# A fused attention, FFN and linear-attention kernel: three edits at the two ends of its first FFN phase

## The reference, cut to what matters

```python
x = x + attn_a(layernorm(x))    # one causal head of width 128, with rope
x = x + ffn(layernorm(x))       # the first FFN
x = x + attn_b(layernorm(x))    # linear attention: 16 heads of width 64
x = x + ffn(layernorm(x))       # the second FFN, same weights

def ffn(x):                     # x_prev is x one token earlier
    xr = mu_r * x + (1 - mu_r) * x_prev
    xk = mu_k * x + (1 - mu_k) * x_prev
    r = sigmoid(xr @ W_r.T)
    k = relu(xk @ W_k.T) ** 2
    return r * (k @ W_v.T)
```

## Time and profile before

| what | us |
|---|---|
| median of the 3 runs | 851.22 |
| all runs | 851.21, 851.22, 853.79 |
| the profiled execution's own time | 855.38 |
| its span | 853.5 |
| attention phase, from the span's start | 0 to about 208.2 |
| first FFN | 208.4 to 251.4 |
| linear phase with the second FFN | 251.7 to the end |
| PE busy over the span | 802.7 (94%) |
| DVE, ACT, POOL busy | 550.5, 558.1, 563.0 |

### The profile page before, as it was taken

How to read it: one execution, slowest core, us unless ns; L and a number is a source line. 1 busy time by engine, 2 the same in 40 slices (tenths; PEclk the granted TensorE clock), 3 DMA queues, 4 the chain that set the end, 5 groups by cost and what they waited for, 6 DMA issues and landing times.

```text
span 853.5 us, 31084 instructions
## 1 busy us (share of the span) xinstructions
PE 802.7 (94%) x13187; PEld 695.4 (81%) x13187; DVE 550.5 (65%) x1267; ACT 558.1 (65%) x1171; POOL 563.0 (66%) x449
## 2 busy tenths in 40 slices
PE   5889999999979999999999999999999999998897
PEld 4668999898867879888888788798888887886786
DVE  4997667674863556656756655666566566674775
ACT  4656555555768667767776767676767767665664
POOL 4971211311528897797797887977977978778361
PEclk9999999999989999999999999999999999999999
DMA  4300000100000000000000000000000000000012
GB/s 142 113 1 20 26 20 8 26 19 11 17 2 1 4 2 2 4 3 3 3 4 3 2 3 3 4 3 3 4 3 3 3 3 3 3 3 3 3 37 62
DMA packets 20423, 12.36 MB, mean 14 GB/s; under 512 B 7872, under 2 KB 19008, under 8 KB 20288
## 3 DMA queue, kind: packets, MB, share of 16 engines
q1 hardware_dynamic: 20288, 10.39, 4.4%
HBM read 8.29 MB, written 2.10 MB: 12 GB/s over the span
## 4 chain that ended last, share of the span: by engine, by line
PE 51%; POOL 7%; ACT 6%; issue 3%; DVE 3%; ACTq 0%; POOLq 0%; DVEq 0%
PE la_ps L1488 8%; PE la_ps L1490 6%; PE la_ps L1489 6%; PE la_o_ps L1551 4%; PE la_o_ps L1567 4%; PE la_s_ps L1581 4%; PE la_ps L1598 3%; PE la_ps L1532 3%; POOL la_scale L2177 3%; ACT la_u_hi L1985 2%; PE la_ps L1519 2%; PE la_ps L1633 2%; PE la_ps L1635 2%; PE la_ps L1634 2%; ACT n_xn L2025 2%
## 5 line engine op out<-in xcount | busy, mean ns | idle before, releaser
L2145 POOL TENSOR_TENSOR la_coef<-la_ssk,lt_mhalf 128x32 f32<-128x32 f32 x16 | 87.1, 5441 | 71.5 <-DVE la_ssk L1815 71.5
L1488 PE MATMUL la_ps<-la_x_hi,w_hi 128*128 128x256 f32 x384 | 116.8, 304 | 1.9 <-ACT la_v L1955 1.0
L1489 PE MATMUL la_ps<-la_x_lo,w_hi 128*128 128x256 f32 x384 | 107.6, 280 | 0.2 <-issue 0.2
L1490 PE MATMUL la_ps<-la_x_hi,w_lo 128*128 128x256 f32 x384 | 107.7, 280 | 0.0
L2177 POOL TENSOR_TENSOR la_scale<-la_scale,lt_mhalf 128x32 f32<-128x32 f32 x16 | 97.4, 6085 | 6.7 <-DVE la_scale L1791 6.7
L1838 DVE TENSOR_TENSOR lt_state<-la_s_ps,la_faded 128x512 f32<-128x512 f32 x62 | 42.6, 686 | 69.8 <-PE la_o_ps L1567 51.9
L1488 PEld LDWEIGHTS la_ps<-la_x_hi,w_hi 128*128 128x128 f32 x384 | 72.4, 188 | 14.2 <-issue 6.2
L530 POOL CAST w_hi<-qkv_w_raw 128x256 fp32r<-128x256 f32 x20 | 7.9, 396 | 109.5 <-PE qkv_xt_ps L573 78.8
L1489 PEld LDWEIGHTS la_ps<-la_x_lo,w_hi 128*128 128x128 f32 x384 | 72.6, 189 | 0.8 <-issue 0.4
L600 PE MATMUL qkv_v_ps<-V,qkv_probsT 128*128 128x128 f32 x544 | 71.9, 278 | 1.0 <-ACT qkv_probsT L706 1.0
L1490 PEld LDWEIGHTS la_ps<-la_x_hi,w_lo 128*128 128x128 f32 x384 | 72.3, 188 | 0.0
(11 more groups left out here) (235 smaller groups left out, 2436.1 us busy)
## 6 DMA issues: line engine op xcount, KB each, us to landing
qkv_w_raw<-in_w SPq DMA_DIRECT2D x20, 128.0 KB, 2.2
X<-in_x SPq DMA_DIRECT2D x8, 256.0 KB, 3.2
out<-X SPq DMA_DIRECT2D x8, 256.0 KB, 2.3
qkv_cos<-in_cos SPq DMA_DIRECT2D x4, 256.0 KB, 3.0
qkv_sin<-in_sin SPq DMA_DIRECT2D x4, 256.0 KB, 3.9
lt_w_out<-in_w_out SPq DMA_DIRECT2D x4, 128.0 KB, 2.7
qkv_w<-in_w_qkv SPq DMA_DIRECT2D x1, 320.0 KB, 3.6
const<-in_const SPq DMA_DIRECT2D x1, 256.5 KB, 4.2
```

Source lines behind the costliest of these rows:

```text
L1488: eng.matmul(out, l_hi, r_hi, start=True, stop=False)
L1489: eng.matmul(out, l_hi, r_lo, start=False, stop=False)
L1490: return eng.matmul(out, l_lo, r_hi, start=False, stop=True)
L2145: eng.tensor_tensor(coef[:, :], ssk[:, :], mhalf[:, :], ALU.pow).then_inc(s["coef_step"], 1)
```

## The change

Three edits, and one that follows from them.

1. DVE computes the moments of groups 2 and 3 of the FFN in the attention phase, after the copies of query tiles 12 and 13 of row 1, and POOL their inverse roots after the weight split of tile 14. In the FFN phase these moments and roots are left out.
2. In slot 8 of the FFN PE computes the keys of group 7 first, then the values of group 6, and the receptance of group 7 last; ACT does `square(7)` ahead of `tanh(7)`.
3. The x of the linear phase's first step is turned in slot 8 of the FFN by PE, ahead of the values of group 7, into the bank `xt_ps[0]`. ACT copies it there, POOL forms its low part there. The new class `LinearInput` holds the three buffers and their semaphores.
4. The linear phase starts at step -1 in place of -2, its ring of banks has one job less, and its first ACT instruction writes `yT` in place of `beta`.

```diff
+FFN_MEASURED = 4
...
         def attend_gpsimd(eng):
...
                         tables.gpsimd_rates(eng)
+                    if b == B - 1 and n == SMALL + 6:
+                        for g in range(2, FFN_MEASURED):
+                            next_norm.inverse_roots(eng, Tile(0, g))
...
         def attend_vector(eng, low_part):
...
                         next_norm.first_normalized(eng)
+                    if b == B - 1 and 2 <= n - SMALL - 2 < FFN_MEASURED:
+                        eng.wait_ge(o_read, (B - 1) * NT + SMALL)
+                        next_norm.moments(eng, Tile(0, n - SMALL - 2))
...
+class LinearInput:
+    def __init__(self, sb, sem):
+        self.xT = sb("la_xT", [P, B * P])
+        self.x_hi = sb("la_x_hi", [P, 2, B * P], F32R)
+        self.x_lo = sb("la_x_lo", [P, 2, B * P], F32R)
+        self.full, self.xt_ready, self.hi_ready, self.xlo_ready = (
+            sem("la_" + n) for n in ("first_full", "xt_ready", "first_hi", "xlo_ready"))
...
 # ffn_phase, POOL
-                if exists(g.later(2)):
+                if exists(g.later(2)) and not has_been_measured(g.later(2)):
                     norm.inverse_roots(eng, g.later(2))
...
             run_slots(eng, slot)
+            eng.wait_ge(first_x.xt_ready, 1)
+            eng.wait_ge(first_x.hi_ready, 1)
+            eng.tensor_tensor(first_x.x_lo[:, 0, :], first_x.xT[:, :], first_x.x_hi[:, 0, :].bitcast(F32),
+                              ALU.subtract).then_inc(first_x.xlo_ready, 1)
...
 # ffn_phase, DVE
-                if exists(g.later(2)):
+                if exists(g.later(2)) and not has_been_measured(g.later(2)):
                     norm.moments(eng, g.later(2))
...
 # ffn_phase, ACT
-                if exists(g.later(-1)):
+                if g.off == GROUPS:
+                    square(g.later(-1))
+                    tanh(g.later(-1))
+                    eng.wait_ge(first_x.full, 1)
+                    eng.activation(first_x.xT[:, :], xt_ps[0][:, 0:B * P], ACT.Copy).then_inc(first_x.xt_ready, 1)
+                    eng.activation(first_x.x_hi[:, 0, :], xt_ps[0][:, 0:B * P], ACT.Copy).then_inc(first_x.hi_ready, 1)
+                elif exists(g.later(-1)):
                     tanh(g.later(-1))
                     square(g.later(-1))
...
 # ffn_phase, PE
+                if g.off == GROUPS:
+                    keys(g.later(-1))
+                    values(g.later(-2))
+                    receptance(g.later(-1))
+                    eng.wait_ge(xt_ready, GROUPS - 1)
+                    eng.wait_ge(next_norm.ready, B)
+                    for b in range(B):
+                        mm = eng.transpose(xt_ps[0][:, b * P:(b + 1) * P], next_norm.xn[:, 0, b * P:(b + 1) * P], ident)
+                    mm.then_inc(first_x.full, 1)
+                    return
...
 # linear_phase
-        STEPS = range(-2, NT + 1)
+        STEPS = range(-1, NT + 1)
...
-                written(eng, *turned(n - 2))
+                if n > 2:
+                    written(eng, *turned(n - 2))
                 norm.normalize(eng, Tile(0, n))
...
-            eng.activation(beta[:, 0:1], const[:, C_LEFT:C_LEFT + 1], ACT.Silu)
+            eng.activation(yT[:, 0:1], const[:, C_LEFT:C_LEFT + 1], ACT.Silu)
```

18 lines of the change are left out of this document (10 added, 8 removed).

## The result

| kernel | median of the runs (lowest to highest) | profiled execution: time, span, mean clock |
|---|---|---|
| before | 851.22 us (850.66 to 853.79, 4 runs) | 855.38, 853.5, 0.989 |
| changed | 845.41 us (844.06 to 846.98, 4 runs) | 844.06, 841.9, 0.996 |

The ratio of the changed kernel's time to the time before is 0.992, with a 95% interval of 0.9899 to 0.9941. That is 6.8 us by the ratio (5.0 to 8.6) and 5.8 us by the medians, where the forecast had 4.0. Measured twice more on other chips, the ratio was 0.9926 [0.9904, 0.9947] and 0.992 [0.9901, 0.9939], and the medians were 5.5 and 6.9 us apart.

A forecast was written before the change was run, and what follows sets the result against it. A chain of waits without slack from the linear phase's start, and PE's waits around the first FFN, were taken as the bound. -1.7 + 0.05 - 0.25 - 1.9, with 0.2 more, took 851.22 to 847.2 us; range 844.9 to 849.9.

The forecast's parts named there:

- Edit 1: FFN start: groups 2 and 3 normalized early, PE's waits go, group 4 normalized 1.65 us sooner; -1.7 us.
- The next bound: FFN: group 4's normalizing waits for POOL's roots behind group 2's low part, beginning near 221.15 where it was 222.79.
- The cost in attention: Moved moments fit into DVE's wait for the scores at tiles 12 and 13; cost 0, bounds 0 and +0.3 us.
- the contention: FFN start: DVE's eight normalizing tiles and POOL's low part of group 0 hinder each other; +0.05 us, bound 0.3.
- Edit 2: FFN end: PE waits 1.05 us for POOL's low part before the keys, the last values start sooner; -0.25 us.
- Edit 3: Linear phase start: keys begin 1.2 us into the block, not 3.08; -1.9 us if the clock falls, -3.4 if not.
- A fall that comes later than before: Linear phase start: a clock fall in the middle of the first keys gives up to 0.5 us more, 0.2 taken.
- Nothing behind the first power: Linear phase's later steps: every engine's list stays the same and all starts move together; no gain counted there.
- The profile's own distance to the median: Whole kernel: the profiled execution lies 4.16 us above the median, unexplained; the same difference was taken for the changed kernel.
- The clock does not fall: Rival at the barrier: PE's shorter rest keeps the clock up; -5.35 us, 845.9 us; chance 0.26.
- Absorbed in part: Rival: in the FFN only PE's listed waits go, in the linear phase half the gain; -1.75, 849.5 us; chance 0.20.
- Slower: Rival in the linear phase: the 16 steps mesh worse, 0.41 us lost per step giving about 854 us; chance 0.04.

The follow-up runs named there:

- no_moments: Changed kernel with the moments and roots of groups 2 and 3 back in the FFN: 848.26 us, ratio 0.9931 to the kernel before.
- only_moments: Kernel before with only the moments and roots of groups 2 and 3 moved into attention: 853.44 us, ratio 0.9989.
- no_order: Changed kernel with the old order in the last FFN slot (receptance, values, keys; tanh ahead of squares): 848.57 us, ratio 0.9942 to the kernel before.
- only_turn: Kernel before with only the linear phase's first x turned in the FFN: 850.47 us, ratio 0.9962.
- before_shift1: Kernel before with one unread multiplication of 16 columns ahead of the FFN's last keys: 852.75 us, ratio 0.9986.
- no_turn: Changed kernel without turning the linear phase's first x in the FFN: 851.78 us, ratio 0.9978 to the kernel before.
- before_again: Kernel before, unchanged, measured and profiled a second time: 853.43 us, ratio 0.9999.

## Why the prediction was right or wrong

**Edit 1** (-1.7, bounds -1.1 and -2.0): 1.57 us off the FFN, by no_moments and by only_moments alike. The next bound was the one named, POOL's roots of group 4 behind the low part of group 2. The cost in attention was 0. For the contention 0.05 was taken; POOL lost 0.08 on the low part, and DVE the rest, 0.97 for eight tiles, where nobody waited for it. The trace agrees with what the prediction cites from the Trainium skill, SBUF — State Buffer, Who interferes with whom, in that the two get in each other's way; the loss of a whole DVE tile by POOL, 0.27 us, was not seen. In the runs the 1.57 us hardly show, by 0.5 us in only_moments and not at all against no_moments: in only_moments' profile, with a fall of the clock behind it, the edit gave 1.03 us back, which the prediction had no term for.

**Edit 2** (-0.25, bounds 0 and -0.6): 0.22 us between no_order and the changed kernel, 0.56 alone. PE stood 0.89 us before the keys where 1.05 was worked out.

**Edit 3** (-1.9 if the clock falls, -3.4 if not): both numbers came out, each in its own executions. The start took 15.07 us on the mean of three old profiles; 13.17 with a fall is 1.9 less, 11.61 without is 3.5 less. The betas and keys began 0.19 and 0.80 us into the block, where 1.2 was worked out for the keys. The second number is right by its mechanism: the first Silu and the square came at 2.01 and 6.61 us, where 2.3 and 6.8 were worked out. The first is right by luck. It took the whole chain to move with the keys under the fall of before, 6.8 us. Where that fall came, in only_turn, 0.7 to 0.8 was gained; the changed kernel got its 1.9 with a fall of half the length. A fall that comes later than before was to give 0.2 more; it gave nothing beyond the 1.9.

**The choice of one branch.** The prediction asked whether the clock falls again and took the likelier case. The same program does both, so the median lies between them. This cost little: up to the first power the mean of three profiles was -4.2 us against the -4.0 of the sum.

**Nothing behind the first power** is the step that failed. The sum ends at the first power. For the steps behind it the prediction had no term, because every engine's list in a step is the same and all starts move together, and it named only a loss there, as a rival. Behind the first power the profiles of the changed kernel are 2.7 us shorter over the fifteen steps (494.36 on the mean of three, 497.02 of two), and 0.8 shorter behind them. About 1.3 us of this is the tenth step, with the pause at 582 us that the change moved away by moving PE's code, as before_shift1 makes likely: one place did it there, and the step took what it takes in the changed kernel. The remaining 2 us are not settled. no_turn has the old start and its pauses at the old places, and its steps were 2.8 us shorter than before's all the same (494.25). And 2 us are no more than what executions of one program differ by in those steps (493.39, 495.99, 493.70), of which I can name two parts. One are further falls of the clock for 3.4 us near 264, 313 and 790 us, which some profiles have; the one at 264 makes the first step 23.4 to 23.6 us in place of 22.8. The other is a wait inside POOL's roots, the same instruction in before and in the changed kernel:

```profile
303.28 1.18 POOL L105 TENSOR_TENSOR n_rstd<-n_mv,n_eps 128x2 f32<-128x2 f32 x1
```

```profile
296.86 0.20 POOL L106 TENSOR_TENSOR n_rstd<-n_mv,n_eps 128x2 f32<-128x2 f32 x1
```

It was short in three profiles of the new start and long in all others, the changed kernel's second among them, and costs its step 0.98 us each time. Over 109 runs of the kernel before the mean granted clock was 0.9920 and the mean time 853.71 us; over the 16 of the changed kernel 0.9953 and 846.56. So the gain of some 7 us goes with less low clock in the runs also, some 5.6 us less of it. At 1.56 us for 3.4 us, what it cost in the first step, that is 2.6 us of the 7, an estimate; how much of it is at the barrier, no single profile tells.

**The profile's own distance to the median**, 4.16 us, was taken off as unexplained. That was sound: before_again's profile, 852.18 us, had the low clock only at the barrier and at the very end, where the first also had it near 61, 317 and 795 us. But part of the 4.16 was the median and not the profile: 851.22 us came from few runs, and beside the experiments the kernel before had medians of 853.13 to 854.19. A sum made against one execution is off by what fell into that execution.

**The rivals.** "The clock does not fall" (845.9) was right for one profile of three and lies nearest to the first measurement, but by luck: the other two profiles had the fall, and the rest of the gain came from behind the first power, which it left out too. "Absorbed in part" did not come about in the changed kernel, but it is what only_moments did, by a mechanism that the prediction did not have: the clock came back later in the block by more than the block had come sooner. "Slower" by steps that mesh worse did not come from the change, yet eight unread instructions did just that, 5.0 us over the fifteen steps (499.40 against 494.36) or 0.3 us per step, by the place of the code, as far as the controls show.
